# Layer 1 of a graph network: one tile in 32 fetched row by row from SyncE and ScalarE

## What is computed

```python
# x: (8192, 128); src, dst: (262144,), dst sorted; edge_attr_9: (262144, 9)
def layer1(x, edge_index, edge_attr, w0, w1, w2, w3, w4):
    i, j = edge_index[0], edge_index[1]                   # src, dst
    summand = tensor_product(x[i], edge_attr, [w0, w1, w2, w3, w4])
    out = segment_sum(summand, j, num_segments=8192)
    return out / sqrt(10.0)

x = layernorm(x + layer0(x, src, dst, edge_weight, W))    # x1 in the kernel
x = layernorm(x + layer1(x, edge_index, edge_attr_9, w0, ..., w4))
```

## Time and profile before

| | us |
|---|---|
| median of 3 runs | 4498.31 |
| lowest and highest | 4495.56, 4499.20 |
| the profiled execution | 4495.43 |
| span of the profile | 4493.6 |
| layer 1, first gather starts to last gather starts | 1869.48 to 4429.01 |
| POOL busy over the span | 2873.1 (64%) |
| PE busy over the span | 3325.0 (74%) |

### The profile page before, as it was taken

One profiled execution on the slowest core, in us unless ns is written; L12 is line 12 of the kernel. 1 busy time (PEld: TensorE's weight loads), 2 busy tenths in 40 slices (PEclk: granted clock), 3 DMA queues, 4 the chain that ended last, 5 costly groups with the idle time before them and its releaser, 6 DMA issues. The chain is left out here.

```text
span 4493.6 us, 78519 instructions
## 1 busy us (share of the span) xinstructions
PE 3325.0 (74%) x21856; PEld 2742.6 (61%) x21858; DVE 2216.3 (49%) x4679; ACT 1222.0 (27%) x1998; POOL 2873.1 (64%) x3027
## 2 busy tenths in 40 slices
PE   2110299999999999677777777777777777777775
PEld 1000299999999999555555555555555565555563
DVE  7999866666666667633333233333332333333324
ACT  4443355555555555310110110101101101011013
POOL 4200176666666666377777777777777777777773
PEclk6555599999999999677777777777777777777776
DMA  1000111111111111322222222222222222222223
GB/s 54 14 0 19 47 51 49 47 49 46 49 48 48 48 48 50 97 56 56 56 56 56 56 56 56 56 56 56 56 56 56 56 56 56 56 56 56 56 56 98
DMA packets 111997, 235.91 MB, mean 52 GB/s; under 512 B 52081, under 2 KB 52225, under 8 KB 110673
## 3 DMA queue, kind: packets, MB, share of 16 engines
q0 software_dynamic: 96560, 200.21, 16.8%
q1 hardware_dynamic: 10658, 24.71, 1.7%
q10 hardware_dynamic: 4608, 8.39, 0.5%
HBM read 218.42 MB, written 8.40 MB: 50 GB/s over the span
## 5 line engine op out<-in xcount | busy, mean ns | idle before, releaser
L1380 POOL DMA_INDIRECT feat<-x,ids x2048 | 1936.6, 946 | 636.4 <-issue 567.8
L991 POOL DMA_INDIRECT l_feat<-in_x,id_of x896 | 848.1, 947 | 746.5 <-ACT w_of L701 347.6
L1444 PE MATMUL quad<-attr_hot,feat 128*128 128x144 f32 x4096 | 988.3, 360 | 415.1 <-DMA feat<-x,ids 409.8
L1535 DVE TENSOR_TENSOR group<-group,quad 128x504 f32 (+1 forms) x512 | 348.1, 680 | 1678.6 <-PE quad L1444 1678.6
L1444 PEld LDWEIGHTS quad<-attr_hot,feat 128*128 128x128 f32 x4096 | 660.2, 216 | 738.8 <-issue 712.8
L1451 PE MATMUL mixed<-group,mix 128*128 128x192 f32 x2304 | 692.9, 486 | 130.7 <-DVE group L1535 130.7
L1451 PEld LDWEIGHTS mixed<-group,mix 128*128 128x128 f32 x2304 | 651.1, 306 | 175.1 <-DVE group L1535 175.1
L1404 ACT CAST ids<-src_col 128x8 int32 x256 | 50.5, 197 | 2293.8 <-DMA feat<-x,ids 2293.8
L1073 PE MATMUL got<-x_near,far_w 128*128 128x128 bf16 x6912 | 481.9, 220 | 1.7 <-ACT far_keys L714 1.1
L1073 PEld LDWEIGHTS got<-x_near,far_w 128*128 128x128 bf16 x6912 | 437.3, 98 | 4.0 <-issue 2.5
L1521 DVE TENSOR_TENSOR attr_hot<-hot,attr_t 128x1152 f32<-128x1152 f32 x256 | 346.7, 1354 | 43.8 <-DVE hot L1515 23.0
(11 more groups left out here) (240 smaller groups left out, 3356.3 us busy)
## 6 DMA issues: line engine op xcount, KB each, us to landing
feat<-x,ids POOLq DMA_INDIRECT x2048, 2.5
l_feat<-in_x,id_of POOLq DMA_INDIRECT x896, 2.5
attr_in<-in_edge_attr SPq DMA_DIRECT2D x129, 72.0 KB
norm_x<-in_x SPq DMA_DIRECT2D x16, 256.0 KB, 2.6
x<-norm_z ACTq DMA_DIRECT2D x16, 256.0 KB, 2.3
norm_x<-x SPq DMA_DIRECT2D x16, 256.0 KB, 2.7
out<-norm_z ACTq DMA_DIRECT2D x16, 256.0 KB, 2.4
keys<-far_keys SPq DMA_DIRECT2D x2, 512.0 KB, 3.2
```

The source lines that it names most:

```text
L991: pool.indirect_dma_start(feat[:, landing % RING, :], None, x, bass.IndirectOffsetOnAxis(ap=id_of[s % 2][:, c:c + 1], axis=0)).then_inc(fe ...
L1380: pool.indirect_dma_start(feat[:, t, :], None, x1, bass.IndirectOffsetOnAxis(ap=ids[t // H][:, t % H:t % H + 1], axis=0),).then_inc(feat_i ...
L1444: nc.tensor.matmul(bank[:, :, bass.ds(off, WIN)], feat[:, t, :], attr_hot[t // H][:, t % H, :, :], start=False, stop=(t % Q == Q - 1), ski ...
L1535: nc.vector.tensor_tensor(to, to, quad[:, q, 0:NA * QUAD_WIN].rearrange("p (m n) -> p m n", m=NA), ALU.add).then_inc(quad_added, 1)
```

## The change

Tile 31 of each pair of rows is no longer gathered by POOL. A new buffer by_row [128, 128] takes it, one row of x1 per transfer. SP issues rows 0 to 71 of the 128 (ROW_PART) and ACT the other 56, in four parts of 14, one behind each of its casts. The row numbers come from ids_row, which holds the source numbers of all such tiles on one partition and is loaded once; `fetch_rows` loads 8 (SP) or 7 (ACT) of them into registers at a time and issues that many transfers. SP opens a turn (`open_rows`): it waits until PE has used the tile before in by_row, clears by_row_in and counts up by_row_open, on which ACT and PE wait. All else of the kernel is as before.

```diff
+        by_row = sb("by_row", [P, D], F32)
+        ids_row = sb("ids_row", [1, RN // 2 * P], I32)
...
+        def fetch_rows(eng, kind, i, first, count, step):
+            for e in range(first, first + count, step):
+                rows = nc.values_load_multi_w_load_instructions(
+                    ids_row[0:1, bass.ds(i * P + e, step)], engines=[kind], min_val=0, max_val=g.N - 1,
+                    skip_runtime_bounds_check_because="every source is the number of a node")[1]
+                for k in range(step):
+                    eng.dma_start(by_row[e + k:e + k + 1, :],
+                                  x1[bass.ds(rows[k], 1), :]).then_inc(by_row_in, 16)
...
+            def open_rows(u):
+                sp.wait_ge(feat_used, u * R + R)
+                sp.sem_inc(g.turn, 1)
+                sp.sem_clear(by_row_in)
+                sp.sem_inc(by_row_open, 1)
+
+            last_tiles = src.rearrange("(i c) -> i c", i=RN // 2)[:, (2 * R - 1) * P:2 * R * P]
+            sp.dma_start(ids_row[:].rearrange("o (i c) -> o i c", i=RN // 2), last_tiles.unsqueeze(0)).then_inc(ids_row_in, 16)
             sp.sem_inc(attr_turned, 2)
             load_attr(0, 0, 0)
+            sp.wait_ge(ids_row_in, 16)
             with passes(sp) as w:
                 with sp.Fori(0, RN // 2 - 1) as i:
                     load_attr(w * RN + i * 2 + 1, i * 2 + 1, 1)
                     load_attr(w * RN + i * 2 + 2, i * 2 + 2, 0)
+                    open_rows(w * RN + i * 2)
+                    fetch_rows(sp, mybir.EngineType.SP, i, 0, ROW_PART, 8)
...
         def _(pool):
             with passes(pool) as w:
-                with pool.Fori(0, RN) as r:
...
+                with pool.Fori(0, RN // 2) as i:
+                    for z in range(2):
...
+                            for t in range(Q * q, Q * q + Q):
+                                if t < R - 1 or z == 0:
+                                    pool.indirect_dma_start(
...
         def _(act):
             act.sem_inc(group_used, 2)
+            act.wait_ge(ids_row_in, 16)
...
                         for h in range(2):
                             for t in range(h * H, h * H + H):
-                                act.wait_ge(feat_in[t], u * 16 + 16)
+                                act.wait_ge(feat_in[t], u * 16 + 16 if t < R - 1 else (w * (RN // 2) + i) * 16 + 16)
                             nc.scalar.copy(ids[h][:], g.src_col[:, bass.ds(r * R + (R + h * H), H)]
                                            ).then_inc(ids_made, 1)
+                            if z == 0 and h == 0:
+                                act.wait_ge(by_row_open, w * (RN // 2) + i + 1)
+                                act.sem_inc(g.turn, 1)
+                            share = (P - ROW_PART) // 4
+                            fetch_rows(act, mybir.EngineType.Activation, i, ROW_PART + (2 * z + h) * share, share, 7)
...
+                                else:
+                                    rows = by_row[:]
+                                    pe.wait_ge(by_row_open, w * (RN // 2) + i + 1)
+                                    pe.wait_ge(by_row_in, 16 * P)
+                                nc.tensor.matmul(bank[:, :, bass.ds(off, WIN)], rows,
```

More of the change, by code:

```diff
@@ L74 @@
 QUAD_WIN = 56
+ROW_PART = 72
 GROUP_WIN = 192
@@ L195, in gnn_kernel @@
         norm_stage(nc, g, "norm0", x, x1, g.w_t[:])
-        layer1(nc, g, x1, attr)
+        layer1(nc, g, x1, attr, src)
         norm_stage(nc, g, "norm1", x1, out, None)
@@ L1300, in offset_in, with layer1 @@
     return (low & (2 ** bits - 1)).with_bounds(min_val=0, max_val=most)
-def layer1(nc, g, x1, attr):
+def layer1(nc, g, x1, attr, src):
     RN, TN = g.RN, g.TN
@@ L1332, in layer1 @@
         attr_here = [sem(f"attr_here{z}") for z in range(2)]
+        ids_row_in = sem("ids_row_in")
+        by_row_open = sem("by_row_open")
+        by_row_in = sem("by_row_in")
         attr_turned = sem("attr_turned")
@@ L1361, in _ @@
                     load_attr(w * RN + i * 2 + 2, i * 2 + 2, 0)
+                    open_rows(w * RN + i * 2)
+                    fetch_rows(sp, mybir.EngineType.SP, i, 0, ROW_PART, 8)
                 load_attr(w * RN + RN - 1, RN - 1, 1)
                 load_attr(w * RN + RN, 0, 0)
+                open_rows(w * RN + RN - 2)
+                fetch_rows(sp, mybir.EngineType.SP, RN // 2 - 1, 0, ROW_PART, 8)
             n_loads = sp.value_load(g.n_pass[0:1, 1:2], min_val=1, max_val=g.PASSES1)
@@ L1371, in _ @@
             with passes(pool) as w:
-                with pool.Fori(0, RN) as r:
[L1373 to L1383, removed]
+                with pool.Fori(0, RN // 2) as i:
+                    for z in range(2):
+                        u = w * RN + i * 2 + z
+                        for q in range(R // Q):
+                            if q % 2 == 0:
+                                pool.wait_ge(ids_made, u * 2 + (q // 2 + 1))
+                            pool.wait_ge(feat_used, u * R + 4 * q + 4)
+                            pool.sem_inc(g.turn, 1)
+                            for t in range(Q * q, Q * q + Q):
+                                if t < R - 1 or z == 0:
+                                    pool.indirect_dma_start(
+                                        feat[:, t, :], None, x1,
+                                        bass.IndirectOffsetOnAxis(ap=ids[t // H][:, t % H:t % H + 1], axis=0),
+                                    ).then_inc(feat_in[t], 16)
             passes_run = pool.value_load(g.n_pass[0:1, 1:2], min_val=1, max_val=g.PASSES1)
             for t in range(R):
-                pool.wait_ge(feat_in[t], passes_run * (16 * RN))
+                pool.wait_ge(feat_in[t], passes_run * (16 * RN if t < R - 1 else 8 * RN))
             pool.sem_inc(g.turn, 1)
@@ L1442, in _ @@
                                 off = offset_in(word, t % Q, TILE_BITS, QUAD_WIN - WIN)
-                                pe.wait_ge(feat_in[t], u * 16 + 16)
-                                nc.tensor.matmul(bank[:, :, bass.ds(off, WIN)], feat[:, t, :],
+                                rows = feat[:, t, :]
+                                if t < R - 1:
+                                    pe.wait_ge(feat_in[t], u * 16 + 16)
+                                elif z == 0:
+                                    pe.wait_ge(feat_in[t], (w * (RN // 2) + i) * 16 + 16)
+                                else:
[3 more added lines that the diff above has]
+                                nc.tensor.matmul(bank[:, :, bass.ds(off, WIN)], rows,
                                                  attr_hot[t // H][:, t % H, :, :], start=False,
```

## The result

| | before | changed |
|---|---|---|
| median of 4 runs each, us | 4497.11 | 4719.03 |
| lowest to highest, us | 4495.56 to 4499.20 | 4716.23 to 4721.78 |
| ratio, with its 95% interval | | 1.0494 [1.0478, 1.0509] |
| span of the profile, us | 4493.6 | 4714.4 |

The changed kernel is 222 us slower. The forecast was 4573, 76 us slower. The sign was right, the size is three times the forecast, just inside the range of 4420 to 4720, and the profile will show that it doesn't come from where the forecast put it.

The account below looks back on a forecast made before the run. POOL's fixed price per gather bounds the kernel now; the change makes SP the bound: 39.1 + 2.1 = 41.2 us a pair, 64 pairs from 1871.3 end at 4508, 75 us more, so 4573 us; range 4420 to 4720.

Parts of the forecast that it names:

- the pace of POOL and what a gather is worth: Layer 1: POOL pays a fixed 1.2486 us per gather; one less per pair gives at most 80 us, 1.8%.
- Rival (a): SP's loop fits under 38.7 us, POOL stays the bound: 4425 us; with pairs up to 39.9, chance 0.31, half near 4425.
- by_row's single buffer makes SP a loop with its way round: SP's 39.1 us of issue plus 2.1 for landing, PE's passes and semaphore: pairs of 41.2 us against 39.95.
- The break-even of 437 ns a row: SP's row price giving a pair of 40.0 us, no gain or loss; the forecast had 454, a margin of 17 ns.
- the start: SP can open its first turn at about 1871.3 us, behind the load of ids_row and its landing.
- the price of an aligned load of eight: On SP: a load of eight row numbers takes 591 ns, from a layer 0 row; 0.71 us with address and gaps.
- What is put on ACT: 14 rows and two loads of seven per half row, 7.6 us; at most 9.6 of 10 with ACT's own work: fits narrowly.
- 0.8 us to spare: ACT's loop: tile 31 to next row's fourth tile 20.1 us after tile 30's gather began; POOL's wait comes at 20.9.
- (b): SP and ACT issues hinder each other or queue up: 3.4 to 7.8 us a pair, 4790 to 5070 us; chance 0.13.
- (c): SP's and ACT's longer loops fetch code anew each turn: 2 us a pair, pairs of 43.2, 4700 us; chance 0.04.
- (d): POOL's time per gather grows to fill the gap left by the removed gather; chance 0.01.
- The test named in the forecast: Trace signs: SP hardly waits for feat_used beyond 1 us; PE waits before tile 31 on SP's rows, not ACT's.

Follow-up runs that it names:

- e17: Changed kernel without any row fetches or PE's two waits, by_row cleared once, tile 31 fetched by nobody: 4425.64 us against 4504.04, ratio 0.9827.
- e16: Changed kernel with 68 rows on SP, 60 on ACT in parts of 20, 16, 16, 8, loads of eight or four: 4433.57 us, ratio 0.9846.
- e18: Changed kernel with ACT's 56 rows in parts of 16, 16, 16, 8 and loads of eight: 4512.18 us, ratio 1.0031.
- e3: Changed kernel with ids_row filled, and every load of row numbers moved, one word further along: 7279.6 us on a held-up chip.
- e8: Changed kernel with 64 rows on SP, 64 on ACT in parts of 24, 16, 16, 8, loads of eight: 4461.6 us, ratio 0.9921.
- e12: Changed kernel with each of ACT's loads of seven starting at a multiple of eight words, from a second copy: 6723.48 us on a held-up chip.
- e4: Same kernel as e17, changed kernel without row fetches, on a held-up chip: 5327.42 us against 5402.78 of the kernel before.
- e2: Same edit of the changed kernel as e8, on a held-up chip: 6247.63 us, ratio 1.1563.
- e1: Same edit of the changed kernel as e18, on a held-up chip: 6625.26 us, ratio 1.2254.

## Why the prediction was right and wrong

**Right: the pace of POOL and what a gather is worth.** The earlier trace rows gave 1.25 us a gather and 80 us at most; e17 gave 78 and e16's pair is 38.7. Rival (a) had +8 us at the end because tile 31 would be used 11.8 us after the last gather and not 3.7; in e16 it is 10.3. (By its own terms (a) is 4428 on the median of the runs; its 4425 is on the profiled run.) That e16 lies 8 us above e17 doesn't show this term: their profiled executions are 2 us apart, 4427.71 and 4425.79.

**Right: by_row's single buffer makes SP a loop with its way round.** e18 is this case, and its pair of 40.06 us stands against 41.2. The terms: eight rows in a row take 3.16 us on SP, so a row is (3.16 - 0.23) / 7 = 0.419 and 72 of them 30.2 us, where 32.7 were forecast, since a one-row transfer issues in 228 ns and not in the 283 of the earlier trace rows (the gaps took back a part: 42 ns each, not 35). The nine loads take 0.81 each with what lies around them ((36.47 - 9 x 3.16) / 8 = 1.00 between two groups of eight, less the 0.19 that belong to a row's pitch), 7.3 us for 6.4. The rest, 40.06 - 30.2 - 7.3 = 2.6 us, is the way round, for 2.1. So -2.5, +0.9, +0.5. The break-even of 437 ns a row was passed by 18 ns, and the loads and the way round took that back: the pair is at the break-even of 40.0.

**Wrong, and small: the start.** By the forecast's sum e18's pair of 40.06 would give 4573 - 64 x 1.14 = 4500 us; it took 4512. The sum had SP open at 1871.3 us, behind the landing of ids_row. In the changed kernel SP opens at 1883.7 and starts its first load of row numbers at 1883.9. In its queue `open_rows` stands behind two `load_attr`, and the second of them (issued at 1883.2) waits until PE has turned the first attributes, which it does from 1881.7 on. Counted back from the last tile 31 (4654.3 - 64 x 43.24), the pairs begin at 1886.9 and not at 1871.3. So the 146 us between forecast and result are 131 of the pair, (43.24 - 41.2) x 64, and 15 of the start.

**Right: the price of an aligned load of eight.** The Trainium skill's rule in "Runtime: NRT & Kernel Launch", Instruction fetch mechanics, of about 200 ns per register even in bulk, is contradicted by the 689 ns of eight on SP, as the forecast said from the earlier trace rows. (The section speaks of registers loaded from HBM; the loads here are from ids_row in SBUF.) But the unaligned eight of e3 takes 1830 ns, which is 229 per register: there the rule agrees. I took the row of 591 ns, which was of a load that starts at a multiple of four, for a price of the call.

**Wrong: "What is put on ACT".** This step ended in "ACT alone would therefore not hold POOL". The true loop of the changed kernel is the one that it priced: tile 31 used, fourth tile of the next row, 14 more gathers, landing of tile 30, ACT's last part, landing, tile 31. Means over the pairs of the trace against the terms of the forecast, in us:

| term | forecast | measured |
|---|---|---|
| tile 31 used (PE's end) to POOL's gather | 8.3 | 9.83 |
| to the gather of tile 30 | 17.5 | 17.49 |
| to ACT's last cast | 2.7 | 3.51 |
| ACT's last part, cast to last issue | 7.6 | 9.65 |
| last issue to PE's end with tile 31 | 1.5 | 2.76 |
| loop | 37.6 | 43.24 |

The size was off by 5.64 us in four terms. (1) The part, +2.0: a seven was priced at 0.67 from an aligned eight and costs 1.14 or 1.73, less what the rows were cheaper. (2) The cast, +0.8: with parts of 9.6 us, a clear of 1.64 every second time and 10 us per half row ACT has no slack left, so that the cast waits for ACT and not for the landing. It is 2.8 in e18 and 4.7 in e8, whose loads are all of eight: this term follows how full ACT's queue is, by loads or by rows. (3) From tile 31 to the gather, +1.5: I took the 8.3 us from one place of the timeline, with a `mixed` of 4.76 us. The trace of the kernel before has others, such as this one:

```profile
2715.48 6.13 PE L1451 MATMUL mixed<-group,mix 128*128 128x192 f32 x18 [1.02 <-DVE group L1535]
```

and over its rows the stretch is 9.0 us on average, not 8.3. In the changed kernel it is 9.0 too, so this is no effect of the change: the row read was a short one. On top come 0.8 us from PE's end to the start of a gather that waits for it (3018.83 + 1.25 = 3020.08, gather at 3020.88), which I had at nothing. (4) The last landing, +1.3: 1.96 us from the end of the issue to PE, and PE's 0.84, against 1.5 in all.

Terms (3) and (4) were wrong in the forecast whatever a load costs: with both put right its own 37.6 us become 40.4. So "0.8 us to spare" was none, and the step should have said that SP's loop and ACT's were within a microsecond of each other. ACT's part then decided which, and by how much: (43.24 - 40.06) x 64 = 204 us, against the 207 that e18 took off. An estimate from these rows for the load alone: with parts of 14 and loads of 0.70 for 1.73 ACT's last part would take 7.6 us and the cast come after 2.8, a loop of 40.5 us on ACT beside 40.06 on SP. So most of the 3.2 us a pair would be the load's; no run shows it by itself.

**Rivals.** (b), SP and ACT in each other's way, did not come: SP's transfers took 227/228/269 ns (least, median, most) beside a burst of ACT (3012.0 to 3019.1) and 228/228/263 with ACT busy clearing (3030.3 to 3033.4). Over the whole trace 2568 of SP's 4608 row transfers overlap one of ACT's, and the median is 228 ns with and without. These are the two stretches of the changed kernel:

```profile
L1359 SPq DMA_DIRECT2D by_row<-x x16: 227/228/269, 3012.0 to 3019.1; - x16
```

```profile
L1359 SPq DMA_DIRECT2D by_row<-x x6: 228/228/263, 3030.3 to 3033.4; - x6
```

By the Trainium skill, "Perfetto Trace Analysis", DMA Instruction — HWDGE, a shared generator was to be expected; for SP and ACT the trace shows no sign of it. (c), code loading, did not come either, though its 43.2 us and 4700 are close to what was measured. The queue that loads code moved what it moved before (a second such queue had 30 packets for 25 in the whole execution):

```profile
q8 instruction: 146, 2.39, 0.2%
```

and e18, with as long a loop, lost 207 of the 222 us. A rival whose number fits is not shown by that. (d) did not come; a gather takes 944 ns.

**The test named in the forecast** was the useful part: "hardly any wait of SP for feat_used beyond 1 us" and "a wait on SP's rows, not ACT's" both failed in the trace of the changed kernel, with 3.9 us a pair, and this is what told a bound on ACT from one on SP.

## What to carry to other kernels

Price a load of registers by its start and its count, and lay the list out so that each load starts at a multiple of four words and takes four or eight: here that, with a small last part, turned 4.9% slower into no more than 0.3%. Where several queues fill one buffer, draw the loop through each of them with all its terms, and take each term as a mean over the stage, not from one place of a timeline. Give the smallest share to the part that comes last, behind the latest event, and move rows between the queues until none of them waits: 72/56, 64/64 and 68/60 gave 4512, 4462 and 4434 us.

## What was not expected of the hardware

- A load of seven registers costs more than one of eight: 1.14 us aligned, 1.73 unaligned, against 0.69 to 0.72; eight unaligned 1.83, four aligned 0.49 to 0.51 (e3, e12, e16). Aligned means here that the load starts at a multiple of four words.
- A transfer of one 512 B row with its row number in a register issues in 228 ns on SP and 232 on ACT, with FUSED_REGOPS of 37 and MOVE of 29, 0.42 us apart on SP and 0.39 on ACT, and beside each other they don't slow down. The first one behind a load of registers takes 263 ns on SP and 466 on ACT.
- 8192 such transfers, with 1088 loads, can be hidden nearly wholly: e16 is within 8 us of a kernel that has none.
- On some chips the engines are held up for about 4 us every 23 or so (e4). It costs 900 us without row fetches and 1790 (e2 against e8) to 2110 (e1 against e18) with them. The number of instructions alone doesn't explain that: those two programs have the same within one. What holds the engines up is open.
